# A shifted-window attention block with a generalised divisive normalisation: a quarter of the attention scores moved to the fourth row tile, keys copied in two stepped transfers

## What is computed

```python
y = roll(ln1(x), (-4, -4))                        # layer norm over the 96 channels
qkv = windows(y, 8) @ qkv_w.T + qkv_b             # windows of 8x8 = 64 tokens
attn = softmax(q * 16**-0.5 @ k.T + mask)         # 6 heads of 16; mask of -100 at the rolled edges
x = x + roll(unwindow((attn @ v) @ proj_w.T + proj_b), (4, 4))
x = x + gelu(ln2(x) @ mlp_w1.T + mlp_b1) @ mlp_w2.T + mlp_b2     # 96 -> 384 -> 96
out = x * rsqrt((x * x) @ gamma_eff.T + beta_eff)
```

## Time and profile before

| | |
|---|---|
| time, median of 3 runs | 2408.51 us (2408.25 to 2411.84) |
| the profiled execution's own time | 2423.21 us |
| its span | 2421.4 us |
| mean granted clock of TensorE | 0.891 of full speed |
| TensorE busy | 1889.1 us (78%) |
| ScalarE busy | 1475.3 us (61%) |
| VectorE busy | 1348.6 us (56%) |
| GpSimd busy | 353.9 us (15%) |
| DMA queue of SP | 101.35 MB in 301080 packets, 18.9% of 16 engines |

### The profile page before, as it was taken

The page is one execution under the profiler, slowest core; times in us unless marked ns, Lnnn a source line. Parts: engine busy times, 40 slices in busy tenths (PEclk is TensorE's granted clock), DMA queues, the critical chain, the costliest instruction groups (busy, mean ns, idle before and its releaser), DMA issues.

```text
span 2421.4 us, 98128 instructions
## 1 busy us (share of the span) xinstructions
PE 1889.1 (78%) x40692; PEld 1616.5 (67%) x40692; DVE 1348.6 (56%) x3502; ACT 1475.3 (61%) x2829; POOL 353.9 (15%) x458
## 2 busy tenths in 40 slices
PE   5688778788778777877877777887787787778786
PEld 3576667677667666766766666676676676667664
DVE  4555555555555565555555555655655655555652
ACT  2466666666666665666666666665666665656665
POOL 1011111111111111111111111111111111111111
PEclk9789989889898998889889999898988888989988
DMA  2122121121122122112112211221221221121111
GB/s 53 30 44 44 43 50 44 44 50 44 43 50 45 42 47 48 42 44 51 43 44 45 47 44 43 50 45 42 50 46 42 48 48 42 45 51 42 43 27 33
DMA packets 302082, 107.74 MB, mean 44 GB/s; under 512 B 153828, under 2 KB 301642, under 8 KB 301642
## 3 DMA queue, kind: packets, MB, share of 16 engines
q1 hardware_dynamic: 301080, 101.35, 18.9%
q10 hardware_dynamic: 562, 0.11, 0.0%
HBM read 32.05 MB, written 25.17 MB: 24 GB/s over the span
## 4 chain that ended last, share of the span: by engine, by line
SPq 86%; issue 8%; PE 3%; DMA 1%; DVE 0%; POOL 0%; ACT 0%; POOLq 0%; DVEq 0%; ACTq 0%
SPq L363 22%; SPq L369 22%; SPq L391 10%; SPq L377 10%; SPq L384 9%; SPq L405 6%; SPq L335 3%; SPq L330 3%; DMA x<-x 1%; PE mm_bank L904 1%; PE score_banks L1034 1%; SPq L238 1%; DMA q<-q 0%; PE mm_bank L902 0%; PE mm_bank L1106 0%
## 5 line engine op out<-in xcount | busy, mean ns | idle before, releaser
L902 PE MATMUL mm_bank<-x_sq,wgdn 97*32 97x384 f32 x768 | 147.7, 661 | 284.8 <-POOL x_sq L485 284.5
L485 POOL TENSOR_TENSOR x_sq<-x 96x512 f32<-96x512 f32 x128 | 132.6, 1036 | 1462.8 <-DMA x<-x 1462.8
L791 DVE TENSOR_REDUCE row_max<-score_banks 128x8 f32<-128x512 f32 x384 | 251.8, 683 | 165.8 <-PE score_banks L1042 99.4
L523 ACT ACT_TABLE_LOAD x256 | 328.4, 1283 | 4.5
L602 ACT ACTIVATE hidden<-mm_bank 128x512 f32<-128x512 f32 x384 | 232.7, 606 | 87.8 <-PE mm_bank L1091 75.9
L608 ACT ACTIVATE log_den<-mm_bank 128x384 f32<-128x384 f32 x128 | 62.8, 490 | 351.3 <-PE mm_bank L904 351.3
L1106 PE MATMUL mm_bank<-hidden,w 128*32 128x128 f32 x2304 | 276.2, 275 | 0.0
L1103 PE MATMUL mm_bank<-hidden,w 128*32 128x384 f32 x2304 | 275.3, 491 | 0.0
L1106 PEld LDWEIGHTS mm_bank<-hidden,w 128*32 128x32 f32 x2304 | 254.8, 111 | 1.8
L799 DVE TENSOR_TENSOR shifted<-score_banks,row_max 128x512 f32<-128x512 f32 x384 | 250.4, 679 | 0.0
L725 DVE BATCH_NORM_STATS2 stats<-turn_banks 128x6 f32<-128x96 f32 x1024 | 181.5, 248 | 106.5 <-PE turn_banks L921 102.3
(11 more groups left out here) (104 smaller groups left out, 5012.5 us busy)
## 6 DMA issues: line engine op xcount, KB each, us to landing
x_ext<-in_x SPq DMA_DIRECT2D x128, 192.0 KB
k_block<-k SPq DMA_DIRECT2D x768, 24.0 KB, 2.1
k_block<-k SPq DMA_DIRECT2D x768, 8.0 KB, 1.8
out<-o_ext SPq DMA_DIRECT2D x64, 192.0 KB
x_ext<-in_x SPq DMA_DIRECT2D x192, 32.0 KB
q<-q SPq DMA_DIRECT2D x384, 16.0 KB, 1.8
attended<-attended SPq DMA_DIRECT2D x384, 16.0 KB, 1.8
x<-x SPq DMA_DIRECT2D x384, 16.0 KB, 1.8
```

The source lines that it names most:

```text
L523: nc.scalar.preload_act_table_set(name)
L791: nc.vector.tensor_reduce(row_max[:, g, :], group_scores(g), op=ALU.max, axis=AX.X)\
```

## The change

The scores now use the strip where it lies. Queries stay in the strip layout and no transfer moves them. The keys are copied in two transfers a half: each takes every second partition (a step of 2, 64 partitions of 384 columns), since the channels of a head pair are now interleaved (`alternating` in the folded weights `wq` and `wk`). The scores run in three steps of eight tiles: three row tiles work on the first six windows as before, the fourth on the last pair of windows of the three head pairs. Its results go to `pv_bank`, so the score groups are four of 384 columns and not three of 512, and the strip's group is first in the softmax (`SOFTMAX_ORDER`). `scores` waits for the division of an earlier half to have read `pv_bank`, and `times_v` waits for the strip group's shift. Input and output use four transfers a unit and not five. SP's list is put in another order (keys first, the output store one round later, x3 before the attended strip), and so is GpSimd's (wrap and bias before the square). `project_v` is not touched by the diff: the 32 small tiles stand between the denominators and the sums before and after.

```diff
+SCORE_GROUPS = GROUPS + 1
+KEY_COPIES = TILE_HEADS
+IMAGE_MOVES = 4
-        k_block = sb("k_block", [DIM, WINDOWS, TILE_HEADS, TOKENS])
+        k_block = sb("k_block", [128, 2, TILE_HEADS, MAIN])
+        SOFTMAX_ORDER = (GROUPS, 0, 1, 2)
...
             def load_x(A):
-                    for j in range(HEAD_PAIRS):
-                        sp.dma_start(x_ext[strip, slot, 2 + 2 * j:4 + 2 * j, 0:WIDTH],
-                                     x[bass.ds(unit // ROWS, 1), group(j), bass.ds(first, 2), :]
-                                     .rearrange("n c h w -> (n c) h w")).then_inc(x_loaded[slot], 16)
+                    for h in range(2):
+                        sp.dma_start(x_ext[strip, slot, 2 + h:WIN:2, 0:WIDTH],
+                                     x[unit // ROWS, :, first + h, :].rearrange("(j c) w -> c j w", c=32))\
+                            .then_inc(x_loaded[slot], 16)
...
             def copy_keys(A):
-                for head in range(HEADS):
-                    sp.dma_start(k_block[rows, first:last - 2, head % TILE_HEADS, :],
-                                 k[rows, A % 2, :].rearrange("c (n t) -> c n t", t=TOKENS))\
-                        .then_inc(keys_copied[A % 2], 16)
+                for e in range(TILE_HEADS):
+                    sp.dma_start(k_block[e:128:TILE_HEADS, A % 2, e, :], k[e:128:TILE_HEADS, A % 2, :])\
                         .then_inc(keys_copied[A % 2], 16)
-                for head in range(HEADS):
-                    sp.dma_start(k_block[rows, last - 2:last, head % TILE_HEADS, :],
...
-            def move_queries(A):
-                wait_alone(sp, q_ready, A + 1)
-                for j in range(HEAD_PAIRS):
-                    sp.dma_start(q[group(j), A % 2, MAIN:HALF], q[strip, A % 2, group(j, 128)])\
-                        .then_inc(q_moved[A % 2], 16)
...
             def steps(run, H):                                     # SP
+                run(copy_keys, QK)
                 run(load_x, TURN_IN + 1)
-                run(copy_keys, QK)
-                run(move_queries, QK)
+                run(store_out, DIVIDE - 1)
+                run(move_x3, SETTLE)
                 run(move_attended, ATTEND - 1)
-                run(move_x3, SETTLE)
-                run(store_out, DIVIDE)
...
             def steps(run, H):                                     # GpSimd
                 run(wrap_out, DIVIDE)
+                run(wrap_x, TURN_IN + 1)
+                run(bias_x2, PROJECT)
                 run(square, SETTLE)
-                run(bias_x2, PROJECT)
-                run(wrap_x, TURN_IN + 1)
                 run(bias_x, TURN_IN)
...
             def scores(A):
-                wait_alone(pe, q_moved[A % 2], 16 * HEAD_PAIRS * (A // 2 + 1))
+                wait_alone(pe, attended_ready, A - 1)
                 wait_alone(pe, keys_copied[A % 2], 16 * KEY_COPIES * (A // 2 + 1))
-                tiles = [(r, n) for r in range(ROW_TILES) for n in range(2)]
-                for p in range(PAIRS):
+                tiles = [(r, n) for r in range(STRIPS) for n in range(2)]
+                for i in range(LAST):
                     for r, n in tiles:
+                        bank = pv_bank[:, cols] if r == GROUPS else score_banks[:, r, cols]
+                        rows, tokens = group(r), group(2 * i + n, TOKENS)
+                        made = nc.tensor.matmul(bank[64 * n:64 * n + 64, :], q[rows, A % 2, tokens],
+                                                k_block[rows, A % 2, :, tokens], start=True,
+                                                stop=mask_kind(A, window_of(A, r, i, n)) is None)
...
             def times_v(A):
                 pe.wait_ge(v_ready, A + 1)
-                wait(pe, attended_ready, A)
+                if has(A + 1):
+                    pe.wait_ge(scores_shifted, softmax_count(A + 1, GROUPS))
...
             def steps(run, H):                                     # VectorE
+                run(max_scores, ATTEND, GROUPS)
                 run(max_scores, ATTEND, 0)
+                run(shift_scores, ATTEND, GROUPS)
                 run(max_scores, ATTEND, 1)
```

More of the change, by code:

```diff
@@ L343, in load_masks @@
                     by_window = kmask.rearrange("m (n h t) -> m n h t", n=WINDOWS, h=HEADS)
-                    for r in range(ROW_TILES):
+                    for r in range(STRIPS):
                         rows = slice(TILE_DIM * r, TILE_DIM * r + QUADRANTS)
@@ L401, in store_out @@
                               (to[:, bass.ds(second, SHIFT), :], o_ext[0:DIM, slot, 4:8, 0:WIDTH])]
-                    stores += [(to[group(j), bass.ds(first, 2), :],
-                                o_ext[strip, slot, 2 + 2 * j:4 + 2 * j, 0:WIDTH]) for j in range(HEAD_PAIRS)]
+                    stores += [(out[unit // ROWS, :, first + h, :].rearrange("(j c) w -> c j w", c=32),
+                                o_ext[strip, slot, 2 + h:WIN:2, 0:WIDTH]) for h in range(2)]
                     for dst, src in stores:
@@ L438, in clear_blocks @@
             def clear_blocks():
-                nc.gpsimd.memset(k_block[:, 0:HALF_WINDOWS, :, :], 0.0).then_inc(pads_cleared, 1)
-                nc.gpsimd.memset(k_block[:, HALF_WINDOWS:WINDOWS, :, :], 0.0).then_inc(pads_cleared, 1)
+                for half in range(2):
+                    nc.gpsimd.memset(k_block[:, half, :, :], 0.0).then_inc(pads_cleared, 1)
             def set_rows():
@@ L568, in softmax_exp @@
             def softmax_exp(A, g):
-                act.wait_ge(scores_shifted, GROUPS * A + g + 1)
-                for bank in ((0, 1), (2,))[g // 2]:
+                act.wait_ge(scores_shifted, softmax_count(A, g))
+                for bank in ((0, 1, 2) if g == GROUPS else (0, 1) if g < 2 else (2,)):
                     wait(act, probs_turned[bank], A)
-                nc.scalar.activation(probs[:, g, :, :, :].rearrange("t p j k -> t (p j k)"),
-                                     shifted[:, g, :, :].rearrange("t i k -> t (i k)"), ACT.Exp)\
-                    .then_inc(probs_ready, 1)
+                dst = probs[:, :, LAST, :, :] if g == GROUPS else probs[:, g, 0:LAST, :, :]
+                nc.scalar.activation(dst, shifted[:, g, :, :].rearrange("t (i e) k -> t i e k", e=TILE_HEADS),
+                                     ACT.Exp).then_inc(probs_ready, 1)
             def probs_t_copy(A, g):
@@ L652, in _, with by_head, alternating, heads_first @@
             row = slice(DIM, DIM + 1)
-            def by_head(values):
+            def by_head(columns):
+                return columns.rearrange("c (j e d) -> c j e d", e=TILE_HEADS, d=HEAD_DIM)
+            def alternating(columns):
+                return columns.rearrange("c (j d e) -> c j e d", e=TILE_HEADS, d=HEAD_DIM)
+            def heads_first(values):
                 return values.rearrange("c (p e d) -> c e p d", e=TILE_HEADS, d=HEAD_DIM)
@@ L669, in fold_qkv @@
                 dve.wait_ge(weights_folded, 4)
-                nc.vector.tensor_scalar(wq[row, :], qkv_bias[row, 0:DIM], head_scale, None,
+                nc.vector.tensor_scalar(alternating(wq[row, :]), by_head(qkv_bias[row, 0:DIM]), head_scale, None,
                                         ALU.mult).then_inc(weights_folded, 1)
-                nc.vector.tensor_copy(wk[row, :], qkv_bias[row, DIM:2 * DIM]).then_inc(weights_folded, 1)
-                nc.vector.tensor_copy(wv[row, :, :, :], by_head(qkv_bias[row, 2 * DIM:3 * DIM])).then_inc(weights_folded, 1)
+                nc.vector.tensor_copy(alternating(wk[row, :]), by_head(qkv_bias[row, DIM:2 * DIM]))\
+                    .then_inc(weights_folded, 1)
+                nc.vector.tensor_copy(wv[row, :, :, :], heads_first(qkv_bias[row, 2 * DIM:3 * DIM])).then_inc(weights_folded, 1)
                 dve.wait_ge(column_sums, 1)
@@ L786, in group_scores @@
             def group_scores(g):
-                return score_banks[:, g, :].rearrange("t (i k) -> t i k", k=TOKENS)
+                bank = pv_bank[:, 0:MAIN] if g == GROUPS else score_banks[:, g, 0:MAIN]
+                return bank.rearrange("t (i k) -> t i k", k=TOKENS)
             def max_scores(A, g):
@@ L794, in shift_scores @@
             def shift_scores(A, g):
-                at = GROUPS * A + g
-                dve.wait_ge(max_ready, at + 1)
-                wait(dve, probs_ready, at + 1 - GROUPS)
+                dve.wait_ge(max_ready, softmax_count(A, g))
+                wait(dve, probs_ready, softmax_count(A - 1, g))
                 nc.vector.tensor_tensor(shifted[:, g, :, :], group_scores(g),
                                         row_max[:, g, :].unsqueeze(2)
-                                        .broadcast_to([128, PAIRS * TILE_HEADS, TOKENS]),
+                                        .broadcast_to([128, LAST * TILE_HEADS, TOKENS]),
                                         ALU.subtract).then_inc(scores_shifted, 1)
```

50 lines of the change are left out of this document (21 added, 29 removed).

## The result

| | before | after |
|---|---|---|
| median of the runs | 2408.38 us (2401.91 to 2411.84, 4 runs) | 2241.58 us (2239.01 to 2246.5, 4 runs) |
| ratio | | 0.9313, 95% interval 0.9287 to 0.9338 |
| the profiled execution: span | 2421.4 us | 2239.0 us |
| mean granted clock | 0.891 | 0.955 |
| DMA packets | 302082 | 179222 |

The change is 6.9% faster. The forecast was 2090 us in a range of 1995 to 2235: the sign is right, the gain is little more than half of the forecast 318 us, and the time lies just above the range.

A forecast was written before the change was run, and what follows sets the result against it. SP's issuing of 26 DMAs a round (18.43 us) was taken as the bound. Steps of 15.5 us plus 0.45 for the clock made 15.93 a round; 127 rounds with head and tail, scaled to the runs, gave 2090 us, range 1995 to 2235.

The forecast's parts named there:

- SP's twelve issues, at 0.71 each: SP's DMA list: 12 transfers a round in place of 26, 8.5 us in all, so SP stops being the bound.
- The x3 strip and the denominators: x3's strip lands 1.1 us before the next scores, so the denominators' wait of 2.2 us a round goes.
- Scores to first maximum, 1.15: From TensorE's scores to VectorE's first softmax maximum: 1.15 us a round in the mean, 1.21 before.
- Inside that step, the fourth row tile: Three score steps in place of four save 0.28 us; masks cost 0.42 us in every second round.
- Steps 2 to 5, the head and the tail: First maximum to normalise 3.70, to values' step 1.05, to projection 1.13, to scores 8.45; first scores 27.7, tail 70.7 us.
- The new wait before the projection: TensorE waits about 1.5 us before the projection for VectorE's eight softmax steps and what follows them.
- The clock, one fall in three rounds: TensorE's clock falls after the projection's wait in one round in three, about 1.3 us each: 0.45 us a round.
- scores no shorter: Rival: the scores, bound by the issue of 48 instructions, do not save 0.28 us; 2125 us; chance 0.13.
- VectorE and the clock at their dear end: Rival: softmax steps above 0.46 us, or clock falls in most rounds; 2160 to 2230 us; chance 0.17.
- Denominators late: Rival: x3's landing or GpSimd's list keeps the denominators' wait of 2.2 us; about 2310 us; chance 0.04.
- TensorE at 1.2 GHz: Rival: the clock stays low between the waits before projection and transposes; slower, about 2440 us at 40% low; chance 0.04.
- does not do what it says: Rival: the values' 32 small tiles stand where they stood, so that part can bring nothing; chance 0.02.

The follow-up runs named there:

- the first experiment: Changed kernel with GpSimd's square and biases put behind VectorE's variance steps: 2077.64 us, ratio 0.8633 to the kernel before.

## Why the prediction was wrong

- *SP's twelve issues, at 0.71 each*: right. They cost 0.58 to 0.62, and SP left the chain. The dear end (2.8 us for a 96 KB copy) is excluded by the 1.15 us of two. The run with 16 key transfers shows that the count alone made the round.
- *The x3 strip and the denominators*: right; the wait of 284.5 us is now 12.1.
- ***Scores to first maximum, 1.15*: the step that failed.** It measured 2.09, and 0.94 x 127 = 119 us of the 152 missed are here. I counted the matmuls and their masks and took for granted that VectorE would be free when they were done. "Other waits" went through the division, the values and ScalarE, and missed the variances at the head of VectorE's softmax. In the kernel before, GpSimd was held up by x3's strip until after them. I wrote that this wait would go and the square come about 0.5 us into the round, and never asked what else runs at that time: bias, square and, in every second round, the input's bias lie on the first variance step, 1.52 us more in the halves without masks (2.59 against 1.07). In the masked halves the hold of 0.81 us costs nothing (1.62 with and without).
- *Inside that step, the fourth row tile*: partly wrong. Without masks the scores are 0.92 us ahead of TensorE's next stage (medians), 0.13 better than the 1.05 before, and not 0.28. With masks they are at 1.50 against 1.27, a loss of 0.24; the three masks cost 0.59, where I took 0.42 and had 0.84 as the dear end. So this quarter of the change brings about nothing in the mean; without the hold the step is 1.35, as against 1.37 before and the 1.15 forecast.
- *Steps 2 to 5, the head and the tail*: right within 0.03 us a step; first scores 28.13 (27.7 forecast), tail 69.1 (70.7).
- *The new wait before the projection*: right in place, 1.82 in place of 1.5 for the reason above; undoing the hold gives 1.1.
- *The clock, one fall in three rounds*: somewhat too small (0.62 in a full round against 0.45), and wrong in reason. Idles of at most 1.6 us before the projection, most of them 1.0 to 1.3, gave no fall, neither here (52 rounds) nor without the hold (115); the rounds with the hold, most of them with about 2.5 us, gave 41 in 53. Without the hold the share is zero, and the forecast of this term too high.
- *From the profiled execution to the runs*: I took 13 us off, since the profiled execution of the kernel before was 0.6% slower than its runs. That of the changed kernel was not (2240.78 against 2241.58).

Of the rivals, *scores no shorter* is right about the scores in the mean (0.13 shorter without masks, 0.24 longer with them), though its 2125 us is far from the result. Its reason, the issue of 48 instructions, is not what the rows show. Without masks the 48 matmuls that the profile lists pass within 0.92 us, at most 19 ns each. The Trainium skill, "TensorE: Matmul & The Clock Gate" (section "Wait — 56ns, not 53.3ns?"), gives a floor of about 25 ns from start to start. The trace disagrees: the 64 listed matmuls of the values start within 0.68 us, 11 ns apart, and 22 if the two entries of each are counted as one. With masks it is the fourth tile that ends last: the other tiles' last matmul starts 0.74 us after the first of the scores (median), the fourth tile's last mask at 1.31. *VectorE and the clock at their dear end* comes nearest in time and names the two right engines, but not the mechanism: the softmax steps start 0.46 to 0.48 us apart, as forecast. *Denominators late*, *TensorE at 1.2 GHz* and *does not do what it says* did not happen. That 2090 us lies near the time without the hold (2077.64) is partly luck. The forecast had 57 us too much for falls of the clock (0.45 x 127), which do not come without the hold; it had 25 us too little in step 1 (0.20 x 127), and the 13 us of the line above should not have been taken off.

## What to carry to other kernels

When a wait goes, the engine that stood in it runs earlier, and every instruction that it now lies beside has to be looked at, also on engines that exchange no semaphore with it. Look for a VectorE instruction with both operands in SBUF beside a GpSimd instruction that reads: it shows as a small instruction that became long, in the busy column and not among the waits. And an edit that brings nothing under one bound (the values' step first: 0.999) can bring 8.8% once the bound is gone, so such edits are worth a second try.

## What the runs showed of the hardware

- One VectorE instruction of 0.17 us with both operands in SBUF took 2.36 us beside two back-to-back GpSimd instructions that read SBUF, and still 0.17 us beside one of 1.77 us that only writes.
- The clock kept its 2.4 GHz level through the single idles of up to 1.6 us before the projection (52 rounds after the change, 115 in the first experiment), although it fell behind 1.47 us before the denominators in the kernel before. And in the run with GpSimd's old order it fell around a projection with 1.08 us before it, where another idle of 1.09 us stood in the values' product just ahead. The length of one idle alone does not decide. Before the projection TensorE has done dense sums and values, before the denominators keys and queries; whether that is the reason was not tried.
- A DMA of 96 KB on 64 partitions with a step costs SP no more to issue (0.58 us) than one of 12 KB (0.72), and it lands 2.0 us after its issue, against 1.8.
